# A graph attention layer and a soft mixture of experts on one core: the chunks of the first attention's products change from 4, 3 and 3 destination tiles to 4, 4 and 2

## The chip, the cores and the metric

The kernel is one program on one core of a Trainium2 chip. Its time is the device time of an execution in microseconds (us). The kernel before was timed in three runs: 1864.38, 1865.25 and 1867.32, median 1865.25 us. A further execution was recorded by the hardware profiler; its own time was 1863.45 us.

## The reference

1,250 nodes carry rows of 768 values. The layers are:

```
x = x + gnn(layernorm(x))      # two graph attention (GAT) layers, relu between
x = x + ffn(layernorm(x))      # soft mixture of 4 experts with 1024 slots each

gat_layer(x, W, att_src, att_dst, bias, src, dst, heads, out_ch):
    h = (x @ W.T).reshape(n, heads, out_ch)
    e = leaky_relu(a_src[src] + a_dst[dst], 0.2)      # a = <h, att> per node and head
    alpha = exp(e - max over edges of dst) / sum over edges of dst
    out[dst] = sum over edges of alpha * h[src]  + bias
```

The first layer has 8 heads of 128 channels, the second one head of 768. There are 41,250 edges (20,000 pairs both ways, and a loop on every node). The change is in the first layer's attention, which is the last two lines of `gat_layer` for 8 heads, with the relu behind it.

## The kernel before

The nodes are padded to 1,280 and cut into ten tiles of 128. The kernel treats the graph as dense: a first stage counts the edges between each destination tile and all sources, and keeps the logarithm of the counts (`ln_c`, one row per destination), so that a softmax over a row of 1,280 sources with that added is the softmax over the edges. Then come the first attention (`attend_heads`), the second layer, the dispatch and the combination of the experts, and the experts' outputs. A barrier of all engines stands between the first attention and the second layer.

`attend_heads` runs 80 steps, `k = head * 10 + j`, one for each head and destination tile j, and some more to drain. In a step:

- GpSimd adds the source's row and `ln_c[j]` into `base` (L838), two buffers.
- ScalarE makes `relu(k + 1)` in PSUM (L848), then the exponential of step k with its sum (L872), then copies the last two turned tiles of step k-1 out of PSUM (L876).
- VectorE adds the two into `q` and takes the maximum (`logits`, L893, L896), then copies the first eight turned tiles of step k-1 to `pt` (L902, two copies).
- TensorE turns step k's 128 x 1280 block by ten transposes (L949), so that sources are on partitions. Its three PSUM banks have one buffer each, so the transposes of step k wait for the copies of k-1.

The attention-weighted sums are products of `h` (stationary, one source tile of the head) with `pt[:, a:a+n, t, :]` (moving: n destination tiles of 128 columns, for source tile t), in 32-bit floats (L962). Ten source tiles are added up in one PSUM bank. A bank holds 512 columns, so the ten destination tiles of a head are cut into three chunks, `DST_CHUNKS`, given as (first tile, number): tiles 0 to 3, 4 to 6 and 7 to 9. Chunk number `g = head * 3 + c` uses the output bank `g % 2`.

`PRODUCTS[j]` writes out by hand which products TensorE does behind the transposes of step j: an entry `(c, back, first, units)` is chunk c of the head `back` heads earlier, `units` source tiles from `first` on. A chunk's products can begin when all its destination tiles have been turned and copied. They run later than the tiles: chunk 0 in steps 4 to 7 of its own head, chunk 1 in steps 8 and 9 and in step 0 of the next head, chunk 2 in steps 1 to 3 of the next head.

What else hangs on the chunks:

- `chunk_ends` has the step in which the chunk's last destination tile is done (3, 6 and 9). In that step ScalarE scales the sums of the chunk (`add_tiny`, L855); in the next, VectorE takes the reciprocals (`inverse`, L910) behind its copies.
- SyncE then turns the reciprocals into a row through memory (`turn_inverse`): a DMA writes them as single elements to `inv_rows` (L815), SyncE waits for it, and a second DMA spreads the row over 128 partitions into `inv[g % 2]` (L821). SyncE does its work in the order written: chunk 0, chunk 1, the load of the `s_row` of two heads on (L808), chunk 2.
- `done_at` has the step in which the chunk's last product runs. Two steps later VectorE multiplies by the inverse and adds the bias with a relu, both in PSUM (`divide`, L917 and L919), and ScalarE takes the high half (`high`, L861); three steps later VectorE takes the low half (`low`, L925). Within a step VectorE's order is logits, copies, inverse, divide, low.
- A chunk's first product waits for the low half of the chunk two before it (same bank), and `inv[g % 2]` is only loaded again once the chunk two before has been divided.

Of the kernel before, what the change touches and what calls it, by code (L numbers as in the profile page):

```python
# [63 lines left out]
THIRD = 418  # L64


DST_CHUNKS = ((0, 4), (4, 3), (7, 3))


PRODUCTS = (  # L70
    ((1, 1, 7, 3),), ((2, 1, 0, 3),), ((2, 1, 3, 4),), ((2, 1, 7, 3),),
    ((0, 0, 0, 3),), ((0, 0, 3, 2),), ((0, 0, 5, 3),), ((0, 0, 8, 2),), ((1, 0, 0, 3),), ((1, 0, 3, 4),),
)


# [51 lines left out]
def build(nc, x, edges, w1t, att1, gb1, w2t, att2, gb2, phi, fw1, fb1, fw2, fb2, out):  # L127
# [8 lines left out]
    def new_part():  # L136
# [8 lines left out]
        "a1": nc.dram_tensor("a1_rows", [HEADS * NT, P], F32).ap(),  # L145
        "inv": nc.dram_tensor("inv_rows", [HEADS * len(DST_CHUNKS), BANK], F32).ap(),
        "a2": nc.dram_tensor("a2_rows", [2, NP], F32).ap(),
# [599 lines left out]
def attend_heads(nc, mem, sem, const, ln_c, h, h1, nad, s_row, in_s, bias_col, in_bias, a_rows, inv_rows):  # L747
# [16 lines left out]
    bias_act = mem("bias_act", [P, HEADS], F32)  # L764
    CHUNK = len(DST_CHUNKS)
    pads, bias_ready = sem("at_pads"), sem("at_bias")
# [9 lines left out]
    def chunk_tiles(g):  # L776
        head, c = divmod(g, CHUNK)
        return head, DST_CHUNKS[c][0], DST_CHUNKS[c][1]


    def slices(k):
        head, j = divmod(k, NT)
        for c, back, first, units in PRODUCTS[j]:
            if 0 <= head - back < HEADS:
                yield (head - back) * CHUNK + c, first, units

    chunk_ends = {(g // CHUNK) * NT + DST_CHUNKS[g % CHUNK][0] + DST_CHUNKS[g % CHUNK][1] - 1: g
                  for g in range(HEADS * CHUNK)}
# [1176 lines left out]
```

## Time and profile before

| what | value |
|---|---|
| median of 3 runs | 1865.25 us |
| profiled execution | 1863.45 us |
| its span, first to last instruction | 1861.6 us |
| TensorE matmul busy | 1716.4 us, 92% of the span |
| VectorE busy | 1116.8 us, 60% |
| ScalarE busy | 857.5 us, 46% |
| GpSimd busy | 266.1 us, 14% (227.5 of it in L838) |
| first attention, first relu to the first work of the next stage | 369.8 to 679.4 us |
| products of the first attention (L962) | 480 matmul passes |
| transposes of the first attention (L949) | 800 |

The shares are averages over the whole kernel. In the first attention all engines are far busier than their shares of the span say, and it is that stage's rows that matter here. A 32-bit product appears as two passes in the profile, each a weight load (PEld) and a matmul (PE). In the timeline, rows that follow each other on an engine and are alike are merged ("x6"), and what stands in brackets is the idle time of the engine ahead of the row, and what ended it. A row's length includes the time in which its result drains, so two rows of one engine can overlap slightly; where the distance of two operations matters, the difference of their starts is used.

### The profile page before, as it was taken

Reading aid. Unit: us, or ns where it says so; the run is one execution under the profiler, and the core shown is the slowest. Engines: PE = TensorE matmul, PEld = TensorE weight load, DVE = VectorE, ACT = ScalarE, POOL = GpSimd, SP = SyncE. Lnnn points to the kernel's source line nnn. Section 1 sums busy time; section 2 is a strip of 40 time slices with the busy share of each in tenths; the row PEclk is TensorE's granted clock in tenths of the full one; section 3 lists DMA queues with packets and bytes.
Section 4 is the critical chain, followed back from the end, with each engine's and each line's share of the span. In section 5 each row is a group of like instructions: output and inputs, shape, how many; then the busy total and the mean of one; then the engine's idle time right before and its main releaser. Section 6 shows DMA issues by size and latency. Waiting matters only on the chain. (4 is left out here: it accounts for less than half of the span.)

```text
span 1861.6 us, 30086 instructions
## 1 busy us (share of the span) xinstructions
PE 1716.4 (92%) x9905; PEld 998.0 (54%) x9905; DVE 1116.8 (60%) x1768; ACT 857.5 (46%) x1358; POOL 266.1 (14%) x116
## 2 busy tenths in 40 slices
PE   3998999779999979989998999999999968999999
PEld 1444444356556546545553555555556545666555
DVE  7997777679999945443222455555555555665301
ACT  2247888688888835421111333333333325555200
POOL 1000000088878805000000000000000000000000
PEclk9999999979999999999999999999999998999999
DMA  6100000011222132030100221111111215440121
GB/s 241 26 1 0 30 0 1 0 25 33 35 48 32 19 82 71 2 126 35 35 26 17 85 67 67 67 67 67 67 67 67 67 73 179 163 145 28 54 68 49
DMA packets 49619, 108.41 MB, mean 58 GB/s; under 512 B 16526, under 2 KB 18664, under 8 KB 49420
## 3 DMA queue, kind: packets, MB, share of 16 engines
q1 hardware_dynamic: 49484, 107.38, 18.8%
q8 instruction: 45, 0.74, 0.2%
q14 instruction: 26, 0.21, 0.1%
q10 hardware_dynamic: 64, 0.08, 0.0%
HBM read 79.02 MB, written 28.43 MB: 58 GB/s over the span
## 5 line engine op out<-in xcount | busy, mean ns | idle before, releaser
L838 POOL TENSOR_TENSOR base<-s_row,ln_c 128x1250 f32<-128x1250 f32 x80 | 227.5, 2845 | 54.5 <-DVE top L893 53.1
L737 PE MATMUL fs<-one_src,one_dst 128*128 x1062 | 211.9, 346 | 23.7 <-ACT one_dst L665 13.7
L93 PE MATMUL di_l<-x2t_hi,ph_hi 128*128 128x512 f16 (+1 forms) x576 | 195.7, 340 | 5.2 <-POOL p L1455 3.8
L94 PE MATMUL di_l<-x2t_lo,ph_hi 128*128 128x512 f16 (+1 forms) x576 | 195.7, 340 | 0.0
L95 PE MATMUL di_l<-x2t_hi,ph_lo 128*128 128x512 f16 (+1 forms) x576 | 195.7, 340 | 0.0
L597 DVE TENSOR_SCALAR one_src<-iota,src 128x1280 f16 x354 | 171.5, 549 | 38.5 <-PE fs L737 31.6
L962 PE MATMUL at_o<-pt,h 128*128 128x384 f32 (+1 forms) x480 | 185.0, 523 | 0.0
L737 PEld LDWEIGHTS fs<-one_src,one_dst 128*128 x1062 | 102.5, 97 | 132.4 <-issue 105.3
L949 PE MATMUL at_t<-ident,q 128*128 128x128 f32 x800 | 107.7, 284 | 29.2 <-ACT q L872 28.5
L93 PE MATMUL co_c<-ps_hi,hid_hi 128*128 128x305 f16 (+1 forms) x384 | 115.5, 301 | 20.8 <-DVE ps_lo L1757 20.1
L949 PEld LDWEIGHTS at_t<-ident,q 128*128 128x128 f32 x800 | 92.5, 145 | 73.8 <-ACT q L872 64.8
L1514 DVE SCALAR_TENSOR_TENSOR pt_lo<-di_t,pt_hi 128x1280 f16<-128x1280 f32 x32 | 47.7, 1492 | 140.5 <-ACT pt_hi L1468 140.5
L662 ACT ACTIVATE apart<-iota,minus_dst 128x128 f16<-128x128 f16 x354 | 115.8, 390 | 31.7 <-PE fs L737 24.8
L848 ACT ACTIVATE at_r<-s_row,nad 128x1250 f32<-128x1250 f32 x80 | 104.5, 1307 | 38.3 <-DVE top L893 36.7
L893 DVE CUSTOM_DVE_ANT_0 q<-at_r,base 128x1250 f32<-128x1250 f32 x80 | 115.8, 1448 | 5.3 <-POOL base L838 3.6
L94 PE MATMUL co_c<-ps_lo,hid_hi 128*128 128x305 f16 (+1 forms) x384 | 115.3, 300 | 0.0
L95 PE MATMUL co_c<-ps_hi,hid_lo 128*128 128x305 f16 (+1 forms) x384 | 115.2, 300 | 0.0
L962 PEld LDWEIGHTS at_o<-pt,h 128*128 128x128 f32 x480 | 85.7, 191 | 53.9 <-issue 23.2
L902 DVE COPY pt<-at_t 128x512 f32<-128x512 f32 x160 | 103.2, 684 | 18.7 <-PE at_t L949 17.4
L872 ACT ACTIVATE q<-q,neg_top 128x1250 f32<-128x1250 f32 x80 | 105.9, 1323 | 0.8 <-DVE neg_top L896 0.8
L93 PE MATMUL di_h<-xw,pt_hi 128*128 (+1 forms) x320 | 104.5, 326 | 1.8 <-DVE pt_lo L1514 1.8
L94 PE MATMUL di_h<-xw,pt_hi 128*128 (+1 forms) x320 | 104.5, 326 | 0.0
(252 smaller groups left out, 3271.4 us busy)
## 6 DMA issues: line engine op xcount, KB each, us to landing
logits_t<-lg SPq DMA_DIRECT2D x32, 625.0 KB, 3.7
logits_in<-logits_t SPq DMA_DIRECT2D x32, 625.0 KB, 4.6
phf<-in_phi SPq DMA_DIRECT2D x32, 384.0 KB, 3.9
s_row<-a_rows SPq DMA_DIRECT2D x9, 640.0 KB, 6.0
ew1f<-in_fw SPq DMA_DIRECT2D x6, 768.0 KB, 5.1
wf<-in_fw SPq DMA_DIRECT2D x12, 384.0 KB, 5.2
xs<-in_x SPq DMA_DIRECT2D x10, 384.0 KB, 4.3
res<-in_x SPq DMA_DIRECT2D x10, 384.0 KB, 3.0
```

Source lines behind the costliest of these rows:

```text
L93: eng.matmul(out, lh, rh, start=first, stop=False, skip_group_check=True)
L94: eng.matmul(out, lh, rl, start=False, stop=False, skip_group_check=True)
L95: return eng.matmul(out, ll, rh, start=False, stop=last, skip_group_check=True)
L597: eng.tensor_scalar(one_src[:, ds(slot(pair, n) + i, 1), :], const["iota"][:, :], src[:, ds(at + i, 1)], None, ALU.is_equal).then_inc(src_ ...
L662: eng.activation(apart[:, n, i, :], const["iota"][:, j * P:(j + 1) * P], ACT.Abs, bias=minus_dst[:, ds(at + i, 1)]).then_inc(apart_ready, 1)
L737: mm = eng.matmul(counts(j)[:, a:a + n], one_dst[:, ds(slot(pair, m) + i, 1), :], one_src[:, ds(slot(pair, m) + i, 1), a:a + n], start=Fal ...
L838: eng.tensor_tensor(base[:, k % 2, 0:N], s_row[:, head % 2, 0:N], ln_c[:, j, 0:N], ALU.add)\
L848: eng.activation(rp[:, 0:N], s_row[:, head % 2, 0:N], ACT.Relu, bias=nad[:, k:k + 1], scale=-0.8).then_inc(relu_ready, 1)
L872: eng.activation(q[:, k % RING, 0:N], q[:, k % RING, 0:N], ACT.Exp, bias=neg_top[:, k:k + 1], accum_out=den[:, k:k + 1]).then_inc(p_ready, 1)
L893: eng.tensor_tensor_reduce(q[:, k % RING, 0:N], rp[:, 0:N], base[:, k % 2, 0:N], 1.0, -MASK / 2, ALU.add, ALU.max, top[:, k:k + 1]).then_i ...
L949: mm = eng.transpose(tp[:, t * P:(t + 1) * P], q[:, k % RING, t * P:(t + 1) * P], const["ident"][:, :])
L962: mm = eng.matmul(op[:, g % 2, 0:n * P], h[:, head, t, :], pt[:, a:a + n, t, :], start=t == 0, stop=t == NT - 1, skip_group_check=True)
```

## The change

The third chunk is cut to two destination tiles and the second grows to four. The products are laid out anew over the steps: chunk 1 has three source tiles in step 8, two in step 9 (5 of 10), and five in steps 0 and 1 of the next head; chunk 2, with half the columns of a full bank, has five source tiles in step 2 and five in step 3.

```diff
-DST_CHUNKS = ((0, 4), (4, 3), (7, 3))
+DST_CHUNKS = ((0, 4), (4, 4), (8, 2))
 
 
 PRODUCTS = (
-    ((1, 1, 7, 3),), ((2, 1, 0, 3),), ((2, 1, 3, 4),), ((2, 1, 7, 3),),
-    ((0, 0, 0, 3),), ((0, 0, 3, 2),), ((0, 0, 5, 3),), ((0, 0, 8, 2),), ((1, 0, 0, 3),), ((1, 0, 3, 4),),
+    ((1, 1, 5, 3),), ((1, 1, 8, 2),), ((2, 1, 0, 5),), ((2, 1, 5, 5),),
+    ((0, 0, 0, 3),), ((0, 0, 3, 2),), ((0, 0, 5, 3),), ((0, 0, 8, 2),), ((1, 0, 0, 3),), ((1, 0, 3, 2),),
 )
```

`chunk_ends` and `done_at` are computed from these, so the steps of `add_tiny`, `inverse`, `divide`, `high` and `low` move with them: chunk 1 now ends with tile 7 (its reciprocals are taken in step 8), and its last product is in step 1 of the next head (divided in step 3, low half in step 4). Chunk 2 keeps its steps (reciprocals in step 0 of the next head, divided in step 5, low half in step 6), and so does chunk 0 (4, 9, and 0 of the next head).

## Rows read from the trace of the kernel before

**Rows 1.** Windows: one head; span, then busy us (count) by engine, clock, DMA.

```profile
480.50:515.76 35.26, 33.71 (x160) 21.37 (x160) 33.10 (x63) 30.92 (x48) 28.48 (x11) 1.00 0.25 38
```

**Rows 2.** Waits of VectorE, 394 to 680 us: total us, times, longest.

```profile
DVE pt L902 <- PE at_t L949: 14.0, 26, 1.6
DVE at_o L917 <- DMA inv<-inv_rows: 13.6, 3, 8.5
```

**Rows 3.** Timeline, steps 6 to 1: start us, us, engine, line, operation.

```profile
505.99 1.31 PE L949 MATMUL at_t<-ident,q 128*128 128x128 f32 x10 [0.59 <-ACT q L872]
...
507.14 2.74 PE L962 MATMUL at_o<-pt,h 128*128 128x512 f32 x6
...
507.97 1.43 DVE L893 CUSTOM_DVE_ANT_0 q<-at_r,base 128x1250 f32<-128x1250 f32 x1
...
509.51 1.31 ACT L848 ACTIVATE at_r<-s_row,nad 128x1250 f32<-128x1250 f32 x1
...
509.72 1.25 PE L949 MATMUL at_t<-ident,q 128*128 128x128 f32 x10
...
510.35 1.29 DVE L902 COPY pt<-at_t 128x512 f32<-128x512 f32 x2 [0.75 <-PE at_t L949]
...
511.56 1.45 DVE L893 CUSTOM_DVE_ANT_0 q<-at_r,base 128x1250 f32<-128x1250 f32 x1
...
512.53 1.25 PE L949 MATMUL at_t<-ident,q 128*128 128x128 f32 x10
...
514.37 0.69 DVE L917 TENSOR_TENSOR at_o<-at_o,inv 128x512 f32<-128x512 f32 x1
...
515.76 1.45 DVE L893 CUSTOM_DVE_ANT_0 q<-at_r,base 128x1250 f32<-128x1250 f32 x1
...
519.18 1.45 DVE L893 CUSTOM_DVE_ANT_0 q<-at_r,base 128x1250 f32<-128x1250 f32 x1
...
520.02 1.31 PE L949 MATMUL at_t<-ident,q 128*128 128x128 f32 x10 [0.31 <-ACT q L872]
```

**Rows 4.** Timeline, steps 1 to 5 of the next head.

```profile
521.17 2.10 PE L962 MATMUL at_o<-pt,h 128*128 128x384 f32 x6
...
525.34 0.56 DVE L917 TENSOR_TENSOR at_o<-at_o,inv 128x384 f32<-128x384 f32 x1
...
526.47 1.45 DVE L893 CUSTOM_DVE_ANT_0 q<-at_r,base 128x1250 f32<-128x1250 f32 x1
...
535.85 0.56 DVE L917 TENSOR_TENSOR at_o<-at_o,inv 128x384 f32<-128x384 f32 x1
```

**Rows 5.** Timeline of SyncE's queue over the same head's end.

```profile
508.08 0.37 SPq L815 DMA_DIRECT2D inv_rows<-factor  x1
...
517.12 0.37 SPq L808 DMA_DIRECT2D s_row<-a_rows  x1
518.71 0.37 SPq L815 DMA_DIRECT2D inv_rows<-factor  x1
528.81 0.32 SPq L821 DMA_DIRECT2D inv<-inv_rows  x1
532.82 0.37 SPq L815 DMA_DIRECT2D inv_rows<-factor  x1
```

**Rows 6.** Timeline, SyncE's queue and VectorE at the last head's end.

```profile
650.42 0.37 SPq L815 DMA_DIRECT2D inv_rows<-factor  x1
...
659.93 1.47 SPq L815 DMA_DIRECT2D inv_rows<-factor  x1
...
670.95 0.32 SPq L821 DMA_DIRECT2D inv<-inv_rows  x1
...
675.19 0.57 DVE L917 TENSOR_TENSOR at_o<-at_o,inv 128x384 f32<-128x384 f32 x1 [3.89 <-DMA inv<-inv_rows]
```

**Rows 7.** All 24 writes (L815), then all 24 loads (L821): time to landing.

```profile
DMA to landing us min/median/max: 6.8/8.4/11.0
...
DMA to landing us min/median/max: 3.0/4.8/9.5
```

## Prediction

> **What bounds the kernel now.** I read four views in this order: the windows (one head by engine), the waits of VectorE, the timeline of two stretches, and SyncE's queue. I call the ten steps of a head 0 to 9, and the three groups of destination tiles c0, c1, c2. Chunk widths are multiples of 128 columns.
>
> One head lasts 35.26 us [rows 1]. TensorE is busy for 33.7 of it, VectorE for 33.1, ScalarE 30.9, GpSimd 28.5: no engine has room, and a head's length is a chain through three of them. The changed products are all in this loop; the other stages contain none of them and start behind a barrier, so a microsecond here is one of the kernel.
>
> The chain, in the reader's rows [rows 3]: the logits of a step start on VectorE (507.97). 1.55 us on, ScalarE starts the next relu (509.51), then the exponential; TensorE can transpose 4.26 us after the logits' start (515.76 to 520.02). The copies of turned tiles start 0.63 to 0.69 behind the transposes (509.72 to 510.35), in the *next* step. So with L the start of logits, these copies begin at the largest of L+1.56, (previous L)+4.95, and the transposes' own start+0.64. From their start the next operation follows 1.20 later (510.35 to 511.56). A step with nothing else is at least 2.89 (logits, then the relu that waits for them; my estimate from 1.55 + a relu of 1.31). Extras on VectorE: a divide of 512 columns 1.39 (514.37 to 515.76), of 384 1.13 (525.34 to 526.47) [rows 3, 4]; low half of 512 columns 0.58 (step 0 lasts 3.42 = 1.56 + 1.20 + reciprocal 0.08 + 0.58), of 384 0.46 by the same subtraction. TensorE: transposes take 1.15 before the products (505.99 to 507.14); six passes of 512 columns take 2.58 (to 509.72), which is 0.427 a pass, two passes a matmul; four passes after transposes give 2.81 (509.72 to 512.53). Six passes of 384 take 2.10 with the tail of the last, 0.323 a pass [rows 4]: cost goes by columns, 0.84 ns each.
>
> With these, the lengths of steps 0 to 9 come out as in the trace: 3.42, 2.89, 4.40, 3.22, 3.02, 4.27, 3.22, 3.02, 3.59, 4.20, sum 35.25. VectorE's pure work is 33.0 of that; the rest are waits for transposes, the longest 0.75 in step 8 (the three 512-column products of step 6 hold up the transposes of step 7) [rows 3]. In the whole stage it waits for them 14.0 us, and for the loaded inverses 13.6 [rows 2].
>
> **The change, part by part.**
>
> *Columns.* A head has 30 matmuls and 12,800 columns before and after; ten of the thirty go from 384 to 512 columns, ten from 384 to 256. TensorE's time is equal if 256 columns cost 2 x 0.213. Bounds: the row nearest to a narrow matmul is the transposes of 128 columns, ten of them, each with a weight load, in 1.25 to 1.31 [rows 3], 0.107 apiece, again 0.84 ns a column; so the low end is nothing. The high end is a weight load that nothing covers, at most another 0.19 a pass (its own length in this trace is under the 0.213): 3.8 a head. I take nothing.
> The Trainium skill speaks against narrow matmuls (*TensorE: Matmul & The Clock Gate*, "Back-to-back issue gap"): pairs of weight load and matmul are spaced 81 ns at 128 columns, not the 56 of one alone. By the page 160 passes of c2 with 25 ns more each would be an estimated 4.0 us of TensorE; even then the steps 2 and 3 would carry only 0.25 each, less than VectorE's 0.7 to spare behind step 3. The transposes above don't show it, so the trace differs from the page here.
>
> *Steps rearranged.* Passes now are, by step: 0: six of 512; 1: four of 512; 2 and 3: ten of 256; 4 to 7 as before; 8: six of 512; 9: four of 512. Step cost on TensorE: 3.73, 2.81, 3.28, 3.28, 3.73, 2.81, 3.73, 2.81, 3.73, 2.81. On VectorE c1 is divided in step 3 (was 2), now 1.39, its low half in step 4 (0.58, was 3); c1's reciprocal is in step 8 (was 7); c2's divide in step 5 is 0.87 and its low half in step 6 0.34, both extrapolated in columns (not below; at most as 384: +0.38 a head, 3 us in all). Working the same chain step by step:
> 0: 3.43. 1: 2.89, but its transposes come 0.30 late behind six passes of 512. 2: copies at L+2.31, so 3.51 (4.40 less the divide would be 3.27). 3: 1.61+1.20+1.39 = 4.20. 4: 1.56+1.20+0.09+0.58 = 3.43. 5: 3.63. 6: 3.11. 7: 3.02. 8: copies at L+2.50 (still held by step 6's products), +1.20+0.09 = 3.79. 9: 4.15.
> Sum 35.16: 0.10 a head less, **-0.7 us** over seven heads. The wait moved out of one step is found again in the other.
>
> *SyncE's queue: the price.* Each group's factors go out to memory as single elements, are waited for, and come back spread; SyncE does this in order, with the load of s_row ahead of c2's. The write lands after 6.8 to 11.0 us, the load after 3.0 to 9.5, median 4.8 [rows 7]. Now: c1's write 508.08, s_row 517.12 (9.04 later), c2's write 518.71, its load 528.81 (11.69 behind s_row; 11.5 to 13.3 in the six heads that have that load) [rows 5]. Landing at 528.81 + 4.8 = 533.6, divide at 535.85 [rows 4]: 2.2 us to spare. Over the six heads, each with its own landing, the spare is 3.2, 4.6, 2.3, 2.2, 4.5, 1.8.
> After the change c1's reciprocal stands behind step 8 in place of 7: 31.01 into the head against 27.46, 3.55 later. s_row is issued that much later (nothing waits for it for a head), and c2's write, which was ready 1.6 behind it, must stay behind it. c2's divide comes 20.22 into the next head, was 20.09. So the spare shrinks by 3.5 each: -0.3, 1.1, -1.2, -1.3, 1.0, -1.7. VectorE stands in divide: **+4.5 us**. Behind that divide are queued step 6's logits, and behind these the relu, transposes, everything. Ends: 0 if the landings come 1.7 sooner, +13 (six times 2.2) if they come as in the worst head plus 0.5.
> Does a smaller write land sooner? c0's writes have 512 elements and take 8.0 as the median of the eight, c1's 384 and take 8.3 (6.8 to 8.9; the range of all is in [rows 7]). I take no difference; and were it by size, c1's third more would cancel c2's third less. The Trainium skill has a reason (*DMA: Bandwidth & Descriptors*, "Anatomy of one DMA"): most of the fixed cost is the receipt for the last byte, longest for HBM. By that nothing changes with size, and this trace agrees.
> c0's write (532.82) is ready 4.0 after c2's load is issued [rows 5]; 0.5 stays. c0's own spare of 3.9 in most heads hides that. c1 keeps 3.5.
>
> *The end of the last head* has no cover. VectorE waits for the loads alone: c1's write went at 650.42, c2's could only go at 659.93, 9.51 behind, landed at 670.95, and the divide began at 675.19 [rows 6]. c1's write now goes behind step 8, at 653.95 (that step's end, 0.05 earlier by the sums above), +3.5, and the rest follows: 663.5, 674.5, divide at 678.7. Four operations on 256 in place of 384 columns give back 0.45: **+3.0**. Ends: -2.7 (shortest landings, 6.8, 8.2 and 3.0) and +5.2 (10, 11.0, 4.9).
>
> Sum: -0.7 + 4.5 + 3.0 = +6.8. The profiled execution took 1863.45 (span 1861.6 and 1.85 around it), so 1870.2; it lies 1.8 under the median of the three runs, so the median should be **1872.0**.
>
> **Rivals.**
> *A, no stall in c2 (about no change).* The landings of c2 come early enough in most heads, since TensorE or ScalarE stretch a step and so the divide is later. For: spares of 4.5 in two heads; a stall leaves slack to the rest. Against: four of six already are under 3.5. -0.7 + 3.0 = +2.3: 1867.5.
> *B, faster.* In the last head c1's and c2's transfers got in each other's way (11.0 for a write with 8.4 as the median, 9.5 for a load with 4.8). If the shift takes them apart, the end gives 2.7 back, and the 1.2 us stall of one c0 (in the 13.6 of [rows 2]) isn't there either: -0.7 - 2.7 - 1.2 = -4.6: 1860.7. It decides if c2's write lands within 9.5 of its issue.
> *C, clearly slower.* SyncE has no slack left: c0's write follows directly on c2's load, as in the last head, and takes 11.0 in place of 8.0; with c0's spare of 3.9 that stalls step 9 where the load is slow too, 0.8 in seven heads: 1877.5.
> *D, narrow matmuls not covered.* 1.9 more in each of steps 2 and 3; after what the slack there takes, 2.8 a head: 1887 with c2's stall covered by it. Against: the transposes.
>
> **How the numbers follow.** Forecast 0.48, A 0.30, B 0.08, C 0.11, D 0.03. Range: 1864.5 (A with an end that costs nothing) to 1879 (C and a little), which leaves out B, D and tails, under 2 in 10. 0.2% (3.7 us) is about what a measurement here can tell from nothing, so the bounds are 1861.5 and 1869. Slower: most of the forecast (0.42), C and D: 0.56. Same: A and the forecast's low end: 0.36. Faster: B: 0.08.
>
> **What would show it.** Step lengths in an unstalled head of 3.43, 2.89, 3.51, 4.20, 3.43, 3.63, 3.11, 3.02, 3.79, 4.15; 256-column passes 0.213 apart; in the waits of VectorE a new row of divides waiting for inverses in step 5 of the first six heads, some 21 us in all in place of 13.6 (4.5 in these heads, the rest at the end), with transposes at about 14 again; s_row's load 3.5 later in its head; the divide of the last c2 at about 679. It is wrong if c2's stalls are absent or over 2 us a head, or if the head without stalls isn't within 0.3 of 35.2.

## The result, and the profile after

The changed kernel took 1879.62 us (median of 4 runs, 1875.67 to 1881.82) against 1865.24 beside it: the ratio is 1.0073, 95% interval 1.0054 to 1.0093. It is slower, as forecast, but by 14.4 us in place of 6.8; the median lies 0.6 above the stated range. The profiled execution took 1881.82 (span 1880.0), 18.4 more than that of before: it is the slowest of the four, and the execution profiled before was a quick one. What follows explains these 18.4.

Windows of two heads of the changed kernel, one without a wait for an inverse and one with, and then the two steps behind that wait (columns as in [rows 1]):

```profile
484.05:519.16 35.11, 33.17 (x161) 21.51 (x160) 32.94 (x63) 30.74 (x48) 28.43 (x11) 1.00 0.25 38
```

```profile
519.16:560.93 41.77, 35.06 (x162) 22.84 (x160) 33.10 (x63) 30.98 (x48) 28.43 (x11) 0.92 0.20 33
...
547.93:551.72 3.79, 2.44 (x11) 2.45 (x12) 2.92 (x6) 3.62 (x5) 3.54 (x2) 0.50 0.36 66
551.72:556.64 4.92, 4.92 (x18) 2.60 (x18) 2.90 (x6) 4.00 (x8) 3.66 (x2) 0.86 0.00 0
```

The first head is 0.15 shorter than [rows 1], with a little less work on VectorE. The second does the same work in 6.66 more, and its granted clock is 0.92. The loss is in heads of this second kind and at the end of the stage; the heads without a wait lose nothing. The waits of VectorE from 394 us to the end of the stage, where [rows 2] had 13.6 and 14.0:

```profile
DVE at_o L917 <- DMA inv<-inv_rows: 25.3, 6, 10.6
DVE pt L902 <- PE at_t L949: 21.6, 27, 2.7
```

SyncE's queue ahead of the wait in the second head (as [rows 5]):

```profile
523.49 0.32 SPq L821 DMA_DIRECT2D inv<-inv_rows  x1
523.91 0.37 SPq L808 DMA_DIRECT2D s_row<-a_rows  x1
524.34 0.42 SPq L815 DMA_DIRECT2D inv_rows<-factor  x1
535.64 0.32 SPq L821 DMA_DIRECT2D inv<-inv_rows  x1
536.15 0.37 SPq L815 DMA_DIRECT2D inv_rows<-factor  x1
```

c2's write stands directly behind s_row (0.43, was 1.6), lands 11.3 later, and its load at 535.64 takes 8.4 to land, at 544.05. The timeline shows what that does:

```profile
541.19 1.25 PE L949 MATMUL at_t<-ident,q 128*128 128x128 f32 x10
...
544.14 0.43 DVE L917 TENSOR_TENSOR at_o<-at_o,inv 128x256 f32<-128x256 f32 x1 [4.69 <-DMA inv<-inv_rows]
...
549.28 2.39 PE L949 MATMUL at_t<-ident,q 128*128 128x128 f32 x10 [5.12 <-ACT q L872]
...
550.43 0.69 DVE L902 COPY pt<-at_t 128x512 f32<-128x512 f32 x1 [0.68 <-PE at_t L949]
...
551.46 3.58 PE L962 MATMUL at_o<-pt,h 128*128 128x512 f32 x6
...
555.52 1.29 DVE L902 COPY pt<-at_t 128x512 f32<-128x512 f32 x2 [1.98 <-PE at_t L949]
```

VectorE stands 4.69 us in c2's divide. TensorE has nothing for 5.12 us and comes back at a clock of 0.50, the 1.2 GHz level: ten transposes take 2.39, six passes 3.58 where [rows 3] has 2.74. VectorE waits for these in steps 7 and 8: 3.79 and 4.92 in place of 3.04 and 3.75. A wait of 4.69 costs 6.7.

The end of the stage (as [rows 6]), first SyncE's queue and then VectorE:

```profile
668.97 0.37 SPq L815 DMA_DIRECT2D inv_rows<-factor  x1
678.17 0.32 SPq L821 DMA_DIRECT2D inv<-inv_rows  x1
678.55 0.43 SPq L815 DMA_DIRECT2D inv_rows<-factor  x1
687.82 0.32 SPq L821 DMA_DIRECT2D inv<-inv_rows  x1
```

```profile
686.59 0.70 DVE L917 TENSOR_TENSOR at_o<-at_o,inv 128x512 f32<-128x512 f32 x1 [10.59 <-DMA inv<-inv_rows]
...
692.84 0.43 DVE L917 TENSOR_TENSOR at_o<-at_o,inv 128x256 f32<-128x256 f32 x1 [3.40 <-DMA inv<-inv_rows]
```

Where the 18.4 us are, head by head (from one logits start of step 0 to the next, in the timelines of both; "clock" is what the steps behind the wait took more than in a head without one):

| stretch | before | after | what |
|---|---|---|---|
| up to head 1 | 409.98 | 409.69 | |
| head 1 | 35.27 | 39.16 | wait 2.62 in c2's divide, clock 1.4 |
| heads 2, 3 | 70.51 | 70.31 | |
| head 4 | 36.56 | 41.77 | wait 4.69, clock 1.9; before had a wait of 1.22 for c0 |
| heads 5, 6 | 70.52 | 70.55 | wait 0.20 |
| head 7, nine steps | 31.06 | 37.38 | wait 3.84, clock 2.5 |
| end, to the next stage's start | 25.48 | 27.67 | waits 10.59 and 3.40 |
| the stages behind | 1182.2 | 1183.5 | |

### The profile page after: what moved, and what is told of

It is laid out like the page before. It is cut to its first block and busy times, and to the rows that moved or that the text cites. A ratio compares the mean times of both kernels' runs of the same rounds, so it can differ in the third digit from the quotient of the medians.

```text
span 1880.0 us, 30086 instructions
## 1 busy us (share of the span) xinstructions
PE 1720.3 (92%) x9905; PEld 1004.5 (53%) x9905; DVE 1115.9 (59%) x1768; ACT 856.6 (46%) x1358; POOL 266.0 (14%) x116
## 5 line engine op out<-in xcount | busy, mean ns | idle before, releaser
L962 PE MATMUL at_o<-pt,h 128*128 128x512 f32 (+1 forms) x480 | 188.5, 531 | 0.0
L848 ACT ACTIVATE at_r<-s_row,nad 128x1250 f32<-128x1250 f32 x80 | 104.5, 1307 | 44.1 <-DVE top L893 43.9
```

The costliest lines, as they stand in the source:

```text
L848: eng.activation(rp[:, 0:N], s_row[:, head % 2, 0:N], ACT.Relu, bias=nad[:, k:k + 1], scale=-0.8).then_inc(relu_ready, 1)
L962: mm = eng.matmul(op[:, g % 2, 0:n * P], h[:, head, t, :], pt[:, a:a + n, t, :], start=t == 0, stop=t == NT - 1, skip_group_check=True)
```

## The experiments

Each ran beside the kernel before on the same chip; the ratio is to that.

**The reciprocal alone, one step late.** The chunks and products of before.

```diff
-    chunk_ends = {... + DST_CHUNKS[g % CHUNK][1] - 1: g
+    chunk_ends = {... + DST_CHUNKS[g % CHUNK][1] - 1 + (g % CHUNK == 1): g
```

> The kernel before with its own chunks of 4, 3 and 3 and its own products; only the sums' scaling and the reciprocals of chunk 1 are done one step later (steps 7 and 8 in place of 6 and 7). Queue theory (the loss comes from SyncE's order: chunk 1's write out later, s_row and chunk 2's write behind it, and VectorE waiting in chunk 2's divide, with TensorE's clock falling behind each long wait): 3.6 us of chunk 2's spare are gone, so about as slow as the changed kernel, 1874 to 1881, with waits of divides for the loaded inverses well over 20 us in all. Rival (the widths and places of the products cost the time): no product is touched, so within 2 us of before, 1863 to 1867.

Measured: 1891.93 us (5 runs), ratio 1.0131 (1.0114 to 1.0148). No product was touched, so the rival falls; the size is 11 us above what the queue theory gave. All seven c2 divides wait (3.33, 0.82, 1.20, 5.30, 0.41, 1.77, 4.64), one of c1 waits 0.54, and the end waits 11.24 and 4.37. The waits of VectorE:

```profile
DVE at_o L917 <- DMA inv<-inv_rows: 33.6, 10, 11.2
DVE pt L902 <- PE at_t L949: 22.7, 31, 2.7
```

Against the changed kernel, its c2 has 384 elements to write in place of 256: these writes land after 11.1 us as the mean of seven, those of the changed kernel after 10.5. So in these two profiles the write of the small third chunk lands 0.6 sooner, and the changed kernel waits less for it (11.4 us in its heads against 17.5). That the size alone makes this difference was argued here and not tested.

**SyncE's order, first try.** The changed kernel; the writes use two semaphores in turn (`inv_kept[g % 2]`), `store_inverse` and `spread_inverse` are the two halves of `turn_inverse`, and a spreading load now also waits until the load before it has landed. The diff shows the order alone.

```diff
-                for c in range(CHUNK):
-                    if c == CHUNK - 1 and head + 2 < HEADS:
-                        load_s(head + 2)
-                    turn_inverse(head * CHUNK + c)
+                store_inverse(g)            # g = head * CHUNK
+                spread_inverse(g)
+                store_inverse(g + 1)
+                if head + 2 < HEADS:
+                    load_s(head + 2)
+                store_inverse(g + 2)
+                spread_inverse(g + 1)
+                spread_inverse(g + 2)
```

> The changed kernel with all its products; only SyncE's order is another: write of chunk 1, load of s_row, write of chunk 2, and then the two spreading loads, each write with its own semaphore. Queue theory: chunk 2's write leaves when its reciprocals are ready (2 us earlier, and 9 us earlier in the last head than it would behind chunk 1's landing), no long waits in a head but by chance, heads of 35.1 to 35.3, the end of the stage about 4 us shorter than in the changed kernel: 1860 to 1866. Rival (products): the order of SyncE changes little, 1875 or more.

Measured: 1871.90 us (12 runs), ratio 1.0027 (1.0017 to 1.0038): 8 us less than the changed kernel, and outside both expectations. Within the heads c2's divide no longer waits, but c1's does, in four of them (2.22, 0.88, 0.77, 2.41): s_row and c1's load both land late, with c2's write between them. At the end of the stage the waits are 9.58 and 0.43. The times to landing of the six loads of s_row, which before were 5.5/6.1/9.2:

```profile
DMA to landing us min/median/max: 8.5/12.3/18.1
```

**Both kernels without the transfers of the inverses.** `turn_inverse` is not called, `inv` is set to ones once; so the kernels leave out the division by the sums.

> The kernel before without the transfers of the inverses: the divide multiplies by ones that are set once, so the outputs of the first attention are not divided by their sums. Both theories: every wait for an inverse is gone (13.6 us in the profile of before, of which some 5 at the end of the stage and 1.2 in one head count): 1858 to 1861, heads of 35.26.

> The changed kernel without the transfers of the inverses (the same part left out: not divided by the sums). It prices the new chunks alone. Queue theory with the step sums of the prediction: 0.7 less over seven heads and some 0.4 less at the end than the kernel before without transfers, so 1857 to 1860, at most 1 us from it. Rival (products cost): 8 us or more above it, 1867 or more.

Measured: 1860.35 us (7 runs), ratio 0.9963 (0.9950 to 0.9976), with the old chunks; 1856.91 us (6 runs), ratio 0.9951 (0.9934 to 0.9968), with the new ones. Neither is slower than before, so the rival that the products cost the time falls. The intervals overlap, so a gain of the new chunks isn't shown by the times; the profiles show one of 0.14 a head. One head of each, old and new chunks:

```profile
447.32:482.57 35.25, 33.71 (x160) 21.38 (x160) 33.10 (x63) 30.91 (x48) 28.47 (x11) 1.00 0.05 19
```

```profile
443.99:479.10 35.11, 33.18 (x162) 21.55 (x160) 32.95 (x63) 30.75 (x48) 28.47 (x11) 1.00 0.06 19
```

Heads 1 to 6 are 35.25 to 35.29 with the old chunks and 35.11 or 35.12 with the new. With the changed kernel at 1879.62, the transfers cost it some 23 us, and the kernel before some 6.

**What a pause of VectorE costs.** From the new chunks without transfers (again no division by the sums); in step 5 of seven heads, ahead of c2's divide, four, one, and one shorter addition (448 columns) whose result nothing reads. The diff is shortened: a condition and a wait of each addition for the one before it are left out.

```diff
+                        for n in range(4):     # long; 1 in the short and the shorter
+                            eng.tensor_tensor(unread[:, :], ln_c[:, 0, 0:1024], ln_c[:, 1, 0:1024], ALU.add)
                     divide(done_at[k - 2])
```

> The changed kernel without the transfers of the inverses (not divided by the sums), and in step 5 of seven heads, ahead of chunk 2's divide, four additions of 1024 columns on VectorE whose result is not read: a pause of some 4.5 us, of known length and with no DMA in it. Clock theory (a long pause costs more than its length, since TensorE stands still and its granted clock then falls): steps 7 and 8 of each such head at 3.8 and 4.4 to 5.5 in place of 3.04 and 3.76, the clock of the head at about 0.92, so 7 x (4.5 + 1.4 to 2.5) = 41 to 49 us over the kernel without transfers, 1898 to 1906. Rival (a pause costs its length; what followed the waits in the changed kernel was the transfers' doing): 7 x 4.5 = 31.5, 1888.

> As the long pause, with one addition (about 1.2 us) in place of four. Clock theory, with the waits of 0.4 to 1.2 us of the kernel with the late reciprocal, after which steps 7 and 8 kept their lengths: 7 x 1.2 = 8.4 over the kernel without transfers and no more, 1864 to 1867, clock 1.00 in these heads. Rival (any pause lowers the clock): 10 us more, 1875.

> As the short pause, whose one addition of 1024 columns took 2.7 us beside GpSimd's work, with 448 columns, so about 1.2 us in each of seven heads (the outputs of the first attention are again not divided by their sums). Clock theory with a bound between 1.2 and 1.8 us (after waits of 0.4 to 1.2 us in the kernel with the late reciprocal step 8 kept 3.75, after one of 1.77 it took 5.43): 7 x 1.2 = 8.4 and nothing else, 1864 to 1867. Rival (every pause costs TensorE's clock): another 1.5 to 2 a head, 1875 to 1880.

Measured: 1919.51 us (4 runs), 1889.51 (4) and 1875.16 (4). The lengths of the pauses were not those expected (6.46, 2.69 and 2.09 by the length of step 5, less its 3.62), so the totals must be read by head. Over 35.12 and the pause, a head with the long pause has 2.5 to 2.8 more, in steps 7 and 8 (44.1 to 44.4 in all), with the short 1.3 to 3.0 (39.14 to 40.78, in every head), with the shorter one nothing in five heads of seven and 1.5 and 1.6 in two. The times agree: seven pauses of 6.46 on the 1856.91 of the kernel without them would be 1902.1 by length alone, and 1919.51 was measured. Windows of one head each; the long pause, a short one, and the two kinds of the shorter:

```profile
499.35:543.66 44.31, 35.91 (x162) 23.16 (x160) 39.38 (x68) 31.00 (x48) 28.47 (x11) 0.88 0.04 15
```

```profile
489.88:530.65 40.77, 36.15 (x162) 23.30 (x160) 35.70 (x64) 30.97 (x48) 28.43 (x11) 0.92 0.05 17
```

```profile
411.74:450.58 38.84, 34.82 (x162) 22.85 (x160) 35.10 (x64) 30.86 (x48) 28.44 (x11) 0.96 0.05 18
450.58:487.79 37.21, 33.18 (x162) 21.53 (x160) 35.01 (x64) 30.87 (x48) 28.46 (x11) 1.00 0.05 18
```

The last column but two is the granted clock: where it is 1.00 the pause costs its length, where it is below it costs 1.3 to 3.0 more. No DMA of an inverse runs here, so the extra in steps 7 and 8 of the changed kernel needs none: it is the clock's. The timeline of before has the same fall in the first steps of the stage:

```profile
378.44 2.40 PE L949 MATMUL at_t<-ident,q 128*128 128x128 f32 x10 [12.17 <-ACT q L872]
```

The rival of the short and shorter pauses (every pause costs the clock) falls with the five heads, and so does the forecast that a short one is free: at 2.7 it never was. The pauses of 1.2 that were meant were not tried; in the kernel with the late reciprocal, waits of 0.41, 0.82 and 1.20 left steps 7 and 8 as they were, and one of 1.77, in a head that had also waited 0.54, did not (step 8: 5.43).

**A write behind a load.** The changed kernel, with one wait more in `turn_inverse`.

```diff
+                if g % CHUNK == 0 and g:
+                    eng.wait_ge(in_inv, 16 * g)
                 eng.dma_start(inv_rows[g, 0:n * P]...     # the write of chunk 0
```

> The changed kernel; SyncE issues chunk 0's write only when chunk 2's load has landed (it was issued 0.5 to 2.6 us behind the load). Collision theory (chunk 2's load lands after 6.7, 8.4 and 9.6 us in three heads because the small elements of the write behind it run beside it): every load of chunk 2 lands within 5.6 us, its divide waits at most 1 us in a head, no loss of clock in steps 7 and 8 from there; chunk 0's write is 3 to 4 us later and uses up its own spare of 3.9, so step 9 may wait about 1 us. 1868 to 1874. Rival (long landings come by chance, or from something else): again two or three of seven between 6 and 10 us, 1876 to 1884.

Measured: 1870.87 us (7 runs), ratio 1.0034 (1.0022 to 1.0045), 8.8 less than the changed kernel (7.3 by the ratios). c2's seven loads land after 4.3, 4.0, 3.7, 4.1, 3.6, 4.8 and 4.8 us (in the changed kernel after 6.7, 3.9, 4.0, 8.4, 3.4, 4.1 and 9.6), and its divide waits once, 0.88. c0's waits once, 2.35. So holding the write back removes the long landings of c2's load, and most of its waits. This speaks for the write close behind the load as what stretches it, in some cases; with three long landings of seven against none of seven, in one profile each, it is not proof. Why in three of seven, and how the 9.6 comes with a write 2.55 behind, stays open. The same is seen elsewhere: of the 24 loads before, those that took 8.0 and 9.5 had a write 0.73 and 0.61 behind, and one more with a write 0.57 behind took 3.0. At the end of the stage, where this run doesn't hold c2's write back from c1's load (0.37 behind), that load took 8.7. Place and time are a rival that wasn't tested: four of the five kernels that transfer in this order have a landing of 8 us or more that begins between 535 and 543 us, and the fifth, this one, has 6.5 at 545.

The data themselves are not late. Windows of the changed kernel behind the last packets of the load issued at 535.64, and of the one issued at 577.41 (the last two columns are the share of the DMA engines and GB/s):

```profile
539.40:544.05 4.65, 4.65 (x19) 2.37 (x17) 0.06 (x1) 1.69 (x4) 1.67 (x1) 1.00 0.00 0
580.70:584.00 3.30, 3.30 (x16) 1.93 (x15) 3.23 (x7) 2.88 (x6) 2.53 (x2) 1.00 0.00 0
```

Both loads have moved everything within 3.8 us of their issue. The second lands at once, at 580.81, the first only at 544.05: nothing moves any more, and the landing alone is late.

**SyncE's order, second try, and the end of the stage.** First: s_row is loaded behind c0's write, where nothing is urgent. The diff is against the first try.

```diff
                 store_inverse(g)
+                if 1 <= head < HEADS - 1:
+                    load_s(head + 1)
                 spread_inverse(g)
                 store_inverse(g + 1)
-                if head + 2 < HEADS:
-                    load_s(head + 2)
                 store_inverse(g + 2)
```

> The changed kernel with all its work; SyncE loads s_row behind chunk 0's write, a quiet place, and writes chunk 2's factors before it waits for chunk 1's. Queue theory: chunk 1's and chunk 2's transfers have nothing large beside them, their divides don't wait but by chance; chunk 0's spare falls from 3.9 to about 2.5. Heads of 35.1 to 35.3, end of the stage as in the run with the early store or better: 1861 to 1866. Rival (any order leaves one chunk late, as the early store did with chunk 1): waits of a few us move to chunk 0's divide in step 9, 1868 to 1875.

Measured: 1861.62 us (11 runs), ratio 0.9982 (0.9973 to 0.9991). Of heads 1 to 6 five are 35.12 or 35.13 and one is 35.32. s_row's loads still take 8.4 to 12.6 us, but no divide of c0, whose load is issued behind them, waits. The waits of VectorE from 394 us to the end of the stage:

```profile
DVE pt L912 <- PE at_t L959: 15.9, 25, 2.4
DVE at_o L927 <- DMA inv<-inv_rows: 10.1, 2, 9.6
```

Both are at the end. So, second, the inverses of c1 and c2 of the last head are made without memory (shortened, the waits are left out):

```diff
+    # ScalarE: each factor along a row; TensorE ahead of c2's products; ScalarE again
+    eng.activation(base[:, 0, m * P:(m + 1) * P], zeros, ACT.Relu, bias=factor[:, at:at + 1])
+    eng.transpose(rp[:, i * BANK + t * P:...], base[:, 0, m * P:(m + 1) * P], ident)
+    eng.activation(inv[:, g % 2, 0:n * P], rp[:, i * BANK:i * BANK + n * P], ACT.Copy)
```

> The same order, and in the last head the inverses of chunks 1 and 2 are not sent through memory: ScalarE spreads each factor along a row, TensorE turns six such tiles (0.7 us), ScalarE copies them out. The wait at the end of the stage (10.6 and 3.4 us in the profile of the changed kernel) goes, and the stage ends with TensorE's last product, as in the kernel without transfers: 1857 to 1861, below the kernel before by 4 to 8 us. If the end of the stage is bound by something else, no more than 1 us from the run with s_row early.

> The kernel before, with its chunks of 4, 3 and 3 and its SyncE order, and only the inverses of the last head's chunks 1 and 2 made by TensorE and ScalarE in place of the transfers. If the gain of the run with s_row early and the turned end is that of the end of the stage, some 4.5 us below the kernel before: 1859 to 1862, and the chunks of 4, 4 and 2 are worth 1 to 3 us more on top. If the chunks matter more, 1863 or more.

Measured: 1857.95 us (5 runs), ratio 0.9964 (0.9950 to 0.9977), the fastest kernel of the study that does all the work; and with only the end changed in the kernel before, 1861.50 (11 runs), ratio 0.9987 (0.9978 to 0.9996). The end of the first, on VectorE:

```profile
664.03 0.70 DVE L959 TENSOR_TENSOR at_o<-at_o,inv 128x512 f32<-128x512 f32 x1 [5.85 <-ACT inv L896]
...
667.87 0.43 DVE L959 TENSOR_TENSOR at_o<-at_o,inv 128x256 f32<-128x256 f32 x1 [0.99 <-PE at_o L1014]
```

c2's divide now waits 0.99 for its products and for nothing else. The kernel with the old chunks still has one wait of 2.48 for a load of c0, in the head in which before had 1.22. That head takes 37.83, 2.57 over 35.26, and the clock stays at 1.00 behind it. The wait of 2.35 in c0's divide of the run with the held write was of about the same length, and there the clock fell to 0.56 behind it and the next head took 1.4 more. So the length of VectorE's wait alone doesn't decide.

## Why the prediction was right in direction and half the size

- **Columns: right.** Ten passes of 256 take 2.20 with what follows them (495.94 to 498.14 in the changed kernel), 0.22 each against 0.213, and a head without waits has the length the sum by columns gave. The wider spacing that the Trainium skill gives for narrow matmuls (*TensorE: Matmul & The Clock Gate*, "Back-to-back issue gap") isn't seen at 256 columns, as the transposes had said for 128.
- **Steps: right.** Forecast and measured (head 3): 3.43/3.42, 2.89/2.90, 3.51/3.52, 4.20/4.20, 3.43/3.42, 3.63/3.62, 3.11/3.12, 3.02/3.04, 3.79/3.76, 4.15/4.12; the sum 35.16/35.11. Over seven heads -1.0 for -0.7.
- **The stall of c2: the place right, the term mis-sized.** "VectorE stands in divide: +4.5 us" is the step that failed; it measured 11.4 (2.62, 4.69, 0.20, 3.84). c2's writes came somewhat sooner than thought (their loads left 11.1 us behind s_row as the mean of six, in place of the 12.3 that the six heads of before give). But the spares were reckoned with the landings of loads as they were before, each with 3 to 6 us free behind it. The later c2 also moved its load directly ahead of c0's write, 0.5 to 0.9 in five heads of seven, and two of these five loads landed late (6.7 and 8.4). With the landings of before in their place, the loads at their measured times would have cost the six heads some 2 us, an estimate from the same rows; the rest of the 11.4 comes from longer landings. The prediction saw the closeness ("0.5 stays", rival C), and priced it at c0's write, not at c2's load. The head without an s_row, which was given no stall, had a landing of 9.6 and a wait of 3.84. The late write of c2 was then shown to be the cause by the late reciprocal alone; the wait for the landing speaks for the collision. Three waits are over 2 us, which the prediction had named as a sign that it is wrong.
- **What follows a stall: not in the prediction.** "Behind that divide are queued step 6's logits, ... everything" counts the wait's own length. TensorE came back at half its clock, 5.8 us over three heads. VectorE's waits for transposes, forecast at about 14 us again, were 21.6. The profile of before had no pause of that length inside a head, but its timeline had the same fall in the first steps, where ten transposes took 2.40 in place of 1.25. In these runs waits of up to 1.2 us cost their length alone, those from 1.8 to 2.5 sometimes more, and those of 2.6 and over, within a head, always.
- **The end: right.** +2.2 for +3.0. c2's write left 9.58 behind c1's, forecast 9.51, and only the transfers bind there, as the turned end shows. Some of the fit is luck: c2's write landed after 9.3 us, where the forecast had taken the 11.0 of before.
- **c0 and c1: right**, neither waited within a head; the 1.22 of before was not repeated.
- **Sum** against the profile: -1.0 + 11.4 + 5.8 - 1.3 + 2.2 = 17.1, and 1.0 in the first head and behind the stage, is 18.1 of the 18.4. The forecast had 6.8. The bound of "+13" on the stall held. The median lies above the range by 0.6, and the 5.8 of the clock, which were in no term, are more than that.

## What to carry to other kernels

A chain of transfers with a few microseconds to spare is not free when the spare is cut to nothing: its mean may still fit, but the long landings, of 7 to 10 us where 4.8 was the median, then stand on the path one by one. Moving one small step (here a reciprocal) moves everything behind it in a queue that is issued in order, so list the pairs that become neighbours in it. And where TensorE is the engine that stands still, price a wait by its length and by the work that follows at the lower clock.

## What was not expected of the hardware

The additions meant as pauses of 1.2 us took 2.77 (1024 columns, both operands in SBUF), and in a row of four only the first did, the others 1.22:

```profile
L929 DVE TENSOR_TENSOR at_unread<-ln_c x28: 1224/1224/2777, 431.3 to 702.3; 128x1024 f32<-128x1024 f32 x28
```

GpSimd's addition of 2.85 us is under way when the first is issued. The Trainium skill (*SBUF — State Buffer*, "Who interferes with whom") says that a VectorE instruction with two inputs in SBUF contends with a GpSimd instruction that reads SBUF; the 1.55 us on the first addition alone agree with it, as GpSimd has nothing to do under the other three. No run took GpSimd's work away, so the cause is not shown.
